# A state-space scan that reads its decays from SBUF and writes its states to PSUM

## The reference

```python
def step(h, inp):
    dt_t, B_t, C_t, u_t = inp
    dA = jnp.exp(dt_t[:, :, None] * A)
    h = h * dA + (dt_t * u_t)[:, :, None] * B_t[:, None, :]
    y = jnp.einsum('bdn,bn->bd', h, C_t)
    return (h, y)
```

## Time and profile before

| | us |
|---|---|
| median of 3 runs | 666.56 (663.95 to 671.63) |
| the profiled execution's own time | 668.15 |
| its span in the trace | 666.3 |
| mean granted TensorE clock | 0.843 of full speed |

### The profile page before, as it was taken

The page is one execution under the profiler, slowest core; times in us unless marked ns, Lnnn a source line. Parts: engine busy times, 40 slices in busy tenths (PEclk is TensorE's granted clock), DMA queues, the critical chain, the costliest instruction groups (busy, mean ns, idle before and its releaser), DMA issues.

```text
span 666.3 us, 7102 instructions
## 1 busy us (share of the span) xinstructions
PE 452.1 (68%) x2352; PEld 376.6 (57%) x2352; DVE 589.3 (88%) x618; ACT 405.9 (61%) x874; POOL 389.4 (58%) x292
## 2 busy tenths in 40 slices
PE   3848687678566756778567856776666956775764
PEld 3637566566465645666456745665665756654642
DVE  4809999999999999999999999999999999999321
ACT  2374756558655868387755866487737774754232
POOL 4066759547855786557845694657746696661100
PEclk9978876898689789889689778989789966877886
DMA  7273042002400070005200160007000240000000
GB/s 214 70 248 122 1 162 92 1 16 78 178 1 0 19 268 1 0 17 179 92 0 13 50 226 1 0 16 260 12 0 1 82 190 0 1 16 1 0 16 17
DMA packets 19870, 44.31 MB, mean 67 GB/s; under 512 B 2348, under 2 KB 11060, under 8 KB 19829
## 3 DMA queue, kind: packets, MB, share of 16 engines
q1 hardware_dynamic: 19832, 43.84, 18.9%
HBM read 41.48 MB, written 2.36 MB: 66 GB/s over the span
## 4 chain that ended last, share of the span: by engine, by line
DVE 58%; issue 14%; PE 11%; ACT 9%; POOL 6%; DMA 1%; DVEq 0%; SPq 0%; ACTq 0%; POOLq 0%
DVE ring L635 33%; DVE hs L639 8%; DVE conv L625 5%; POOL hs L383 4%; PE YT L940 3%; ACT ring L504 3%; PE PY L983 2%; DVE st L605 2%; DVE yt L646 2%; DVE kmax L682 2%; PE PX L901 1%; ACT L455 1%; PE PX L836 1%; PE PY L1024 1%; ACT L578 1%
## 5 line engine op out<-in xcount | busy, mean ns | idle before, releaser
L383 POOL TENSOR_TENSOR hs<-dtu,BC 128x1024 f32<-128x1024 f32 x128 | 299.7, 2358 | 107.8 <-PE YT L940 107.7
L635 DVE TENSOR_TENSOR_SCAN ring<-ring,hs 128x1024 f32<-128x1024 f32 x128 | 292.1, 2282 | 20.2 <-POOL hs L383 16.2
L504 ACT ACTIVATE ring<-dt,Aneg 128x256 f32<-128x256 f32 x512 | 213.2, 464 | 149.2 <-DVE hs L639 149.1
L940 PE MATMUL YT<-ident,hs 128*128 128x128 f32 x1024 | 160.0, 312 | 51.5 <-DVE hs L639 51.4
L940 PEld LDWEIGHTS YT<-ident,hs 128*128 128x128 f32 x1024 | 139.9, 163 | 67.6 <-DVE hs L639 62.5
L639 DVE TENSOR_TENSOR hs<-ring,BC 128x1024 f32<-128x1024 f32 x128 | 156.8, 1225 | 4.4
L901 PE MATMUL PX<-xnT,win 128*128 128x256 f32 x232 | 67.0, 439 | 27.2 <-ACT xnT L435 11.2
L901 PEld LDWEIGHTS PX<-xnT,win 128*128 128x128 f32 x232 | 48.8, 222 | 39.9 <-ACT xnT L435 13.6
L983 PE MATMUL PY<-wqkvo,xT 128*128 128x256 f32 x192 | 63.3, 489 | 0.0
L983 PEld LDWEIGHTS PY<-wqkvo,xT 128*128 128x128 f32 x192 | 49.5, 258 | 10.2
L362 POOL TENSOR_TENSOR dt<-dt,conv 128x512 f32<-128x512 f32 x16 | 20.3, 1271 | 53.0 <-ACT conv L484 53.0
(11 more groups left out here) (126 smaller groups left out, 601.4 us busy)
## 6 DMA issues: line engine op xcount, KB each, us to landing
BC<-bc_rows SPq DMA_DIRECT2D x32, 1024.0 KB, 10.1
xg<-in_x SPq DMA_DIRECT2D x8, 256.0 KB, 2.8
out<-fin SPq DMA_DIRECT2D x8, 256.0 KB, 12.3
BC<-in_ada_wT SPq DMA_DIRECT2D x3, 512.0 KB, 5.0
win<-in_in_wT SPq DMA_DIRECT2D x2, 512.0 KB, 6.7
BC<-in_W_emb SPq DMA_DIRECT2D x2, 512.0 KB
wo<-in_out_wT SPq DMA_DIRECT2D x1, 512.0 KB, 13.0
bc_rows<-xdbl SPq DMA_DIRECT2D x8, 32.0 KB, 1.5
```

What stands on the lines that cost most here:

```text
L383: nc.gpsimd.tensor_tensor(hs[:, g % DBUF], dtu[:, b % 2, dc, :].unsqueeze(1).to_broadcast([P, NQ, T]), BC[:, b % 2, NQ * q:NQ * q + NQ, :] ...
L504: ins = nc.scalar.activation(ring[:, g % 2, j, :], dt[:, b % 2, dc, :], ACT.Exp, scale=Aneg[:, c:c + 1])
L635: V.tensor_tensor_scan(states, states, driven, 0.0, ALU.mult, ALU.add).then_inc(s_scan_done, 1)
L940: ins = M(YT[:, c, :], hs[:, g % DBUF, j, P * c:P * c + P], ident[:, :], is_transpose=True, start=False, stop=(q == UPC - 1 and j == NQ - ...
```

## The change

The decays get a tensor of their own in SBUF, da, with ABUF = 2 buffers of 1024 columns. The exponentials write there, and wait for the scan of unit g - 2 (s_scan_done) instead of the multiplication. The scan reads decays from da and the input from hs, both SBUF, and writes the states into ring in PSUM; the scan of unit 0 also waits until silu_z has read the ring. To make room in SBUF, three buffers become other names of existing ones: xnT is xhat, qT is xT, kT is xh. Waits are added or changed for that in normalize0, normalize2 and copy_qT.

```diff
-DBUF, XBUF = 5, 3
+DBUF, XBUF, ABUF = 5, 3, 2
...
-        xnT = sb("xnT", [P, KD, T])
+        xnT = xhat
...
+        da = sb("da", [P, ABUF, NQ, T])
         hs = sb("hs", [P, DBUF, NQ, T])
...
-        qT, kT = sb("qT", [P, KD, T]), sb("kT", [P, TC, D])
+        qT, kT = xT, xh
...
             def normalize0(b):
                 act.wait_ge(s_rs0_ready, 2 * b + 2)
                 if b >= 1:
-                    act.wait_ge(s_xT_mm, b)
+                    act.wait_ge(s_xz_mm, 4 * b)
...
-                if g >= 2:
-                    act.wait_ge(s_hc_ready, g - 1)
+                if g >= ABUF:
+                    act.wait_ge(s_scan_done, g - ABUF + 1)
                 for j in range(NQ):
                     c = N * dc + NQ * q + j
-                    ins = nc.scalar.activation(ring[:, g % 2, j, :], dt[:, b % 2, dc, :], ACT.Exp,
+                    ins = nc.scalar.activation(da[:, g % ABUF, j, :], dt[:, b % 2, dc, :], ACT.Exp,
                                                scale=Aneg[:, c:c + 1])
...
             def normalize2(b):
                 act.wait_ge(s_rs2_ready, 2 * b + 2)
-                act.wait_ge(s_x1T_mm, b + 1)
+                act.wait_ge(s_att_mm, b + 1)
...
             def copy_qT(b):
                 act.wait_ge(s_qT_mm, b + 1)
+                act.wait_ge(s_v_mm, b + 1)
...
                 dve.wait_ge(s_dbu_ready, g + 1)
+                if g == 0:
+                    dve.wait_ge(s_z_ready, 3)
                 driven = hs[:, g % DBUF].rearrange("p n t -> p (n t)")
+                decays = da[:, g % ABUF].rearrange("p n t -> p (n t)")
                 states = ring[:, g % 2].rearrange("p n t -> p (n t)")
-                V.tensor_tensor_scan(states, states, driven, 0.0, ALU.mult, ALU.add).then_inc(s_scan_done, 1)
+                V.tensor_tensor_scan(states, decays, driven, 0.0, ALU.mult, ALU.add).then_inc(s_scan_done, 1)
```

## The result

The changed kernel takes 753.64 us (median of 4 runs, 750.61 to 755.98) against 669.1 us for the kernel before in the runs beside it (663.95 to 672.19). The ratio is 1.127, 95% interval 1.120 to 1.133: slower by 12.7%. The forecast was 737 us, 70 us more than before; the loss in the runs is 84.5.

A forecast was written before the change was run, and what follows sets the result against it. VectorE's summed instructions were taken to bound the kernel. With scans and GpSimd taking turns, 558 plus 70 plus 10 made 638 us for 568; 668.15 + 70 = 738, less 1.6 for the runs' median, gave 737, range 672 to 800.

The forecast's parts named there:

- Direction and cause: Whole kernel: slower, chance 0.85, as the scan's two SBUF inputs contend with GpSimd's reading.
- full turns: Stretch of scans: scan and GpSimd's multiplying run one after the other, 638 us in place of 568; chance 0.73.
- rows of kmax: VectorE's negation of kmax: 158 ns at its shortest, 1974 in the median, one seen waiting for a GpSimd product to end.
- the small GpSimd operation: A 128x2 GpSimd operation, 0.27 us in the mean, that ran from 7.41 to 8.63, ending just behind a VectorE SBUF pass.
- Rival (a): Scan beside GpSimd: no conflict at the scan's slow rate, 662 to 667 us, not slower; chance 0.13.
- rival (b): Scan beside GpSimd: they share, GpSimd slowed but not the scan; both slowed a little, 670 to 700; chance 0.09.
- Rival (c): Unfair turns: GpSimd takes two or three products in a row while VectorE's scan stands; halfway 790 to 860; chance 0.05.
- The hand-over: Scan and product turns: 4.65 us a unit, less 0.29 because whoever waits has its start behind it, so 4.36.
- GpSimd's other work: GpSimd's work besides products in the stretch of scans: 42 to 70 us of turns, taken as 70.
- The waste: Around VectorE's long sections away from scans, GpSimd may lack a free buffer: 0.4 us for each of 24, 10 us.
- Parts 1 to 3: Exponentials freed earlier: 0, bounds -4 and 0; scan's own length: 0, within 4 us; aliases and their waits: 0.

The follow-up runs named there:

- number 1: The changed kernel with decays back in the PSUM ring and the scan in place, aliases and their waits kept: 666.94 us, ratio 0.999 to the kernel before.
- number 2: The changed kernel with the scan's input taken from the PSUM ring (zeros), decays still read from SBUF: 665.76 us, ratio 0.996 to the kernel before.
- number 3: The changed kernel with GpSimd's product replaced by a memset of the same 1024 columns: 668.5 us, ratio 0.998 to the kernel before.
- Number 9: The changed kernel without GpSimd's residual and its wait for the gate: 733.33 us, ratio 1.100 to the kernel before.
- number 10: The changed kernel with decays in PSUM again and states written to SBUF, so the multiplication has two SBUF inputs: 742.56 us, ratio 1.116 to the kernel before.
- number 11: The kernel with states in SBUF and a two-SBUF-input multiplication, plus a wait starting each product after an earlier multiplication: 700.35 us, ratio 1.046 to the kernel before.

## Why the prediction was right, point by point

- **Direction and cause** held. The forecast was +70 us, measured is +84.5. The step that chose full turns from the rows of kmax and of the small GpSimd operation is borne out by the lines after and by numbers 1 to 3: two SBUF inputs at VectorE and a reader at GpSimd, no one of them alone. (The rows of kmax were of an operation with one input; that it stands for the same reason as the scan was an argument, and no run tests it.) Rival (a) falls with the scans' 2929 ns, rival (b) too: the product is not slowed evenly but stands, and so does the scan. Rival (c) isn't seen: 85 scans were held for more than 0.06 us, and each ended 2.15 to 2.16 us after the one GpSimd instruction that was running when it started; the longest is 4.37 us.
- **The hand-over** was put at 4.36 us a unit. Summed over single instructions of the trace, a held scan ends 2.154 us after its holder in the median, a held product 2.152: 4.31.
- **GpSimd's other work** at its full 70 us was the right end. Its two-column operations do take turns: line 346, 0.22 us before, is recorded with 1.69 in the mean, so it stands for 1.5 of them.
- **The waste** is the term that was mis-sized. I put 10 us of time in which nobody takes a turn and placed it at VectorE's long sections, where GpSimd would lack a free buffer. Measured is 29 us, and 655.0 - 29.1 = 626 is what is left for the turns (with the last multiplication, 1.2 us), against 628 predicted. The place was in part another: GpSimd waited only 9.8 us for buffers, but 28.5 us for the gate before its residual, because its order is fixed. It had gone as far ahead as slot 24 allows, and stood there while VectorE ran scan, multiplication and gate with nobody beside it, 1.77 us of it empty in each of six batches, 10.6 in all. The wait was in the trace of before, too (42.9 us at line 389), hidden by VectorE's bound. Number 9 shows the residual to be worth 18 us, 9 of them emptiness. The rest of the 29 us, by the single instructions: 7.4 in five gaps in the first two batches, 4.7 behind the last product, where only scans and multiplications are left, and some 6 in short gaps between turns. No run tests these.
- **Parts 1 to 3** held: exponentials at 497 ns, VectorE no longer waiting for them, unheld scans at 2.29 us, aliases free (number 1), the stretches ahead and behind at 48.5 and 46.8 us.
- The remaining difference: the stretch of scans grew by 86.8 us where 70 had been predicted, and the stretch behind it shrank by 2.6 (46.80 against 49.40, at a granted clock of 0.86 against 0.81). The runs of before beside it were 2.5 us slower than those the prediction started from.

The Trainium skill ("SBUF — State Buffer", section "Who interferes with whom") states the rule that a VectorE instruction with two SBUF inputs contends with a GpSimd instruction that reads SBUF, and not with one that only writes it. The scans' mean of 2929 ns beside products and the memset of 951 ns inside a scan agree.

## What to carry to other kernels

Before giving a VectorE operation its second SBUF input, look at what GpSimd reads meanwhile: the two then take turns by whole instructions, and the floor of the loop becomes the sum of both, here 4.3 us a unit where 3.46 had been. For the scan and the multiplication, one operand in PSUM avoided it altogether (numbers 1 and 2). An operation with a single SBUF input isn't always free of it: the negation of kmax is recorded with 1.97 us in the median and 0.16 at its shortest. If it can't be avoided, put the double read where the partner is idle and set the partner's start by a wait, since here the phase made much of what was lost above the floor (1.116 against 1.046, numbers 10 and 11); and look in the trace for tiny operations with a median far above their minimum, which can show, as here, that such turns are already being taken.

## What the runs showed of the hardware that I had not expected

- An instruction that stands behind the other engine is recorded as busy for all of that time (4.36 us for a scan of 2.29), so that GpSimd's 81% and VectorE's 90% are not work.
- The one who stood needs a little less than its plain length once its turn comes: 2.15 us instead of 2.29 for the scan, 2.15 instead of 2.36 for the product.
- A scan at 2.2 ns a column, twice the time of an ordinary operation, keeps a reading GpSimd out for as long as it lasts: a product that began 0.03 us behind it ended 2.15 us after it.
- The contention is as real for an ordinary multiplication (number 10: 1939 ns in the mean for 1224), and its price hung on the phase: the ratio was 1.116, and 1.046 with one more wait (number 11).
